# Queries of the next attention core made within the tail of the feed-forward layer before it, and the norm there applied by ScalarE

## The reference, cut to what matters

```python
x = x + tanh(g_xattn[n]) * xattn_n(layernorm(x), ctx)
x = x + tanh(g_ffn[n]) * ffn_n(layernorm(x))
```

## Time and profile before

| | us |
|---|---|
| median of 3 runs | 2401.34 (2396.65 to 2404.51) |
| the profiled execution | 2401.41 |
| its span in the trace | 2399.6 |
| mean granted TensorE clock, share of 2.4 GHz | 0.952 |
| layer 0's feed-forward part: last products end / stage ends | 412.8 / 449.1 |
| layer 2's feed-forward part: last products end / stage ends | 1819.4 / 1833.5 |

### The profile page before, as it was taken

The page is one execution under the profiler, slowest core; times in us unless marked ns, Lnnn a source line. Parts: engine busy times, 40 slices in busy tenths (PEclk is TensorE's granted clock), DMA queues, the critical chain, the costliest instruction groups (busy, mean ns, idle before and its releaser), DMA issues.

```text
span 2399.6 us, 31201 instructions
## 1 busy us (share of the span) xinstructions
PE 2253.9 (94%) x11544; PEld 1565.3 (65%) x11544; DVE 1542.5 (64%) x2508; ACT 1063.7 (44%) x1561; POOL 1397.2 (58%) x887
## 2 busy tenths in 40 slices
PE   6889999899999996698999999989998999999988
PEld 5677887766666653465566665577886666666576
DVE  4666652478788756666778878652224788788652
ACT  3443343355555544311455555443333555555443
POOL 0342200178888875266688888823443788888743
PEclk9899999799999997799899999999998999999989
DMA  1025564211111113100111111022211111111010
GB/s 35 21 67 161 162 194 137 60 40 39 58 39 39 45 54 108 38 1 9 50 59 39 40 58 39 7 78 85 86 34 52 39 39 43 55 39 46 24 39 16
DMA packets 49842, 136.48 MB, mean 57 GB/s; under 512 B 7470, under 2 KB 13438, under 8 KB 49245
## 3 DMA queue, kind: packets, MB, share of 16 engines
q1 hardware_dynamic: 49308, 134.16, 18.3%
q10 hardware_dynamic: 384, 0.33, 0.1%
HBM read 121.26 MB, written 13.21 MB: 56 GB/s over the span
## 4 chain that ended last, share of the span: by engine, by line
PE 83%; DVE 7%; ACT 3%; POOL 3%; DMA 1%; issue 1%; POOLq 0%; ACTq 0%; SPq 0%; DVEq 0%
PE psum L881 21%; PE psum L1315 19%; PE psum L1305 10%; PE psum L1286 10%; PE psum L1307 10%; PE psum L1488 2%; PE psum L1332 2%; PE psum L1443 2%; DMA V<-in_ctx 1%; PE psum L1411 1%; PE psum L1199 1%; PE psum L1511 1%; PE psum L1088 1%; PE psum L1278 1%; PE psum L1108 1%
## 5 line engine op out<-in xcount | busy, mean ns | idle before, releaser
L1741 ACT ACTIVATE E<-psum 125x896 f32<-125x896 f32 x576 | 528.3, 920 | 584.5 <-PE psum L1307 557.9
L2277 DVE TENSOR_REDUCE mx<-psum 128x1 f32<-128x500 f32 x945 | 611.9, 675 | 172.5 <-PE psum L1286 170.6
L2028 POOL TENSOR_TENSOR SA<-SA,E 125x896 f32<-125x896 f32 x282 | 596.9, 2117 | 22.1
L1315 PE MATMUL psum<-E,V 125*64 125x448 f32 x2304 | 472.2, 545 | 0.0
L1305 PE MATMUL psum<-Q,K 128*125 128x448 f32 x1152 | 331.8, 369 | 2.3 <-ACT E L1741 2.3
L1286 PE MATMUL psum<-K,Q 128*128 128x500 f32 x945 | 329.8, 403 | 2.1 <-DVE Q L2217 1.9
L1307 PE MATMUL psum<-Q,K 128*125 128x448 f32 x1152 | 329.9, 367 | 0.0
L1315 PEld LDWEIGHTS psum<-E,V 125*64 125x64 f32 x2304 | 152.9, 136 | 228.5 <-issue 223.2
L2028 POOL TENSOR_TENSOR SA<-SA,SB 125x896 f32<-125x896 f32 x93 | 194.0, 2086 | 154.6 <-DVE SB L2300 154.6
L1286 PEld LDWEIGHTS psum<-K,Q 128*128 128x128 f32 x945 | 174.7, 188 | 133.9 <-DVE Q L2217 32.6
L1305 PEld LDWEIGHTS psum<-Q,K 128*125 128x125 f32 x1152 | 213.2, 187 | 37.1 <-ACT E L1741 6.9
(11 more groups left out here) (308 smaller groups left out, 3703.6 us busy)
## 6 DMA issues: line engine op xcount, KB each, us to landing
K<-kt_scratch SPq DMA_DIRECT2D x48, 750.0 KB, 4.9
K<-kt_scratch SPq DMA_DIRECT2D x48, 375.0 KB, 6.1
EW<-in_f_w SPq DMA_DIRECT2D x64, 256.0 KB, 6.5
kt_scratch<-kt SPq DMA_DIRECT2D x16, 750.0 KB, 4.4
WS<-in_f_w SPq DMA_DIRECT2D x31, 384.0 KB, 5.2
WoT<-in_a_WoT SPq DMA_DIRECT2D x24, 256.0 KB, 2.6
V<-in_ctx SPq DMA_DIRECT2D x16, 375.0 KB
Wq<-in_a_Wq SPq DMA_DIRECT2D x16, 256.0 KB, 3.0
```

The costliest lines, as they stand in the source:

```text
L1315: i = e.matmul(psum[c * DC:(c + 1) * DC, 4 + b % 2, 0:HT], V[0:LP, b, k * DC:(k + 1) * DC], E[g[n, b, k] % NE][0:LP, half[c]], start=k == ...
L1741: e.activation(E[m % NE][0:LP, :].rearrange("p (c q) -> p c q", c=2), psum[0:LP, pair:pair + 2, 0:HT], ACT.Exp).then_inc(exp_set.sem, 1)
L2028: e.tensor_tensor(SA[b % 2][0:LP, :], a[0:LP, :], x[0:LP, :], ALU.add).then_inc(sum_set.sem, 1)
L2277: e.tensor_reduce(mx[:, b % 2, j * 3 + c:j * 3 + c + 1], psum[:, bank, 0:CW], AX.X, ALU.max).then_inc(small_free.sem, 1)
```

## The change

- Core 1 and core 3: the eight makes of c = 0 move out of the core's order into the tail of the feed-forward part before. There they cover the first three token tiles (384 columns), and the eight that stay in the core cover the other four (512 columns; `MADE`). In the tail they use banks 0 and 2, which are free once `OT` has been copied. Make 0 waits for tile 2's `YL`; make mt waits for its folded weights and for ScalarE's copy of make mt - 2.
- The norm in these two tails is applied by ScalarE (`act_norm`: scale and shift by token), with the shift computed by VectorE and GpSimd (`pool_scales` in place of `pool_rstd`), as the other norms of the kernel are.
- Layer 0's tail follows a table, `TAIL`: ScalarE copies both halves to `OT` first (task `ot`), then folding steps, `back`, `stats` (one tile each), `apply`, `norm` and `make` take turns.
- Layer 2's tail: the turns of tiles 0 to 2, 3 and 4, then makes 0 to 3, the turns of tiles 5 and 6, then makes 4 to 7.
- `act_exp_first` runs behind the copy of `OT`'s second half, in the tail.

```diff
--- before.py
+++ after.py
@@ -193,7 +193,7 @@
                 order += side.pop(0)
             if c == 1 and n + 2 < blocks:
                 order.append(("split", n + 2))
-    return order + [("back", 1)]
+    return order + [("back", 1)] + ([("make", mt, 0) for mt in range(4, H // 2)] if blocks == NB2 else [])
 
 
 def folding_ahead():
@@ -255,12 +256,13 @@
             elif g == NG - 1:
                 order += last.pop(0)
     assert not side
-    order.append(("comb", E0 // 2 - 1))
-    for n, task in enumerate([("back", 0), ("back", 1)] + [("norm", i) for i in range(NT)]):
-        for _ in range((3, 3, 3, 1, 1, 1, 1, 1, 1)[n]):
-            order += last.pop(0) if last else []
-        order.append(task)
-    return order + [t for step in last for t in step]
+    order += [("comb", E0 // 2 - 1), ("ot", 0), ("ot", 1)]
+    for folds, tasks in TAIL:
+        for _ in range(folds):
+            order += last.pop(0)
+        order += tasks
+    assert not last
+    return order
 
 
 def core_order(merged):
@@ -270,10 +272,8 @@
 
 
     units = [(j, c) for j in range(NT) for c in range(3)]
-    makes = [("make", 0, mt, c) for c in range(2) for mt in range(H // 2)] if merged else []
-    order = makes[:H // 2]
-    makes = makes[H // 2:]
-    order += [("queries", 0, n) for n in range(6)]
+    makes = [("make", 0, mt, 1) for mt in range(H // 2)] if merged else []
+    order = [("queries", 0, n) for n in range(6)]
     order += makes[:2]
     makes = makes[2:]
     for j in range(NT):
@@ -350,6 +350,11 @@
     return order + [t for step in fold for t in step]
 
 
+TAIL = [(4, [("back", 0), ("stats", 0)]), (1, [("stats", 1)]), (1, [("back", 1), ("stats", 2)]), (1, [("apply", 0), ("stats", 3)]),
+        (1, [("apply", 1), ("norm", 0), ("stats", 4)]), (1, [("apply", 2), ("norm", 1), ("stats", 5)]),
+        (1, [("apply", 3), ("norm", 2), ("stats", 6)]), (1, [("apply", 4), ("norm", 3)]), (1, [("make", 0, 0), ("apply", 5), ("norm", 4)]),
+        (1, [("make", 1, 0), ("apply", 6), ("norm", 5)]), (1, [("make", 2, 0), ("norm", 6)]), (1, [("make", 3, 0)]),
+        (3, [("make", mt, 0) for mt in range(4, H // 2)])]
 SETUP = [("fm", 0), ("turn", 0), ("turn", 1), ("fa", 0), ("turn", 2), ("turn", 3), ("fm", 1), ("turn", 4), ("turn", 5), ("fa", 1), ("turn", 6)]
 FOLD_LOADS = ("fload_r", "fload_m", "fload_a")
 FOLD_BUFS = {1: 4, 2: 1, 3: 1}
@@ -367,6 +372,7 @@
 EARLY_UP = {2: 5, 3: 4}
 LOGITS_BEHIND = {0: 2, 1: 0, 2: 3, 3: 6}
 TURNED_NORM = {0: 1, 2: 5, 3: 8}
+MADE = (slice(0, 3 * P), slice(3 * P, T))
 BACK = {0: ((0, 1), (2,)), 1: ((3, 4), (5, 6))}
 TURNS = {0: (), 1: ((0, 1, 2), (3, 4), (5, 6))}
 
...
@@ -709,7 +715,7 @@
     fm_made, mh_set, ml_set = (flag(n, fm0 + done(folds, "fm")) for n in ("fm_made", "mh_set", "ml_set"))
     fa_made, ah_set, al_set = (flag(n, fm0 + done(folds, "fa")) for n in ("fa_made", "ah_set", "al_set"))
     q_tiles = [(0, mt, c) for mt in range(H // 2) for c in range(2)]
-    q_tiles += [(n, *t[2:]) for n in (1, 3) for t in CORES[n] if t[0] == "make"]
+    q_tiles += [(n, mt, c) for n in (1, 3) for c in range(2) for mt in range(H // 2)]
     q_made, q_set = flag("q_made", q_tiles), flag("q_set", q_tiles)
 
 
@@ -1142,11 +1148,21 @@
                                 t.then_inc(fa_made.sem, 1)
 
     def make_queries(e, n, mt, c, bank):
-        pairs = []
+        pairs, x = [], half[c] if n == 0 else MADE[c]
         for kd in range(KD):
             o = slice(mt * P, (mt + 1) * P)
-            pairs += split_pairs(AH[:, kd, o], AL[:, kd, o], YH[:, kd, half[c]], YL[:, kd, half[c]])
-        product(e, psum[:, bank, 0:HT], pairs).then_inc(q_made.sem, 1)
+            pairs += split_pairs(AH[:, kd, o], AL[:, kd, o], YH[:, kd, x], YL[:, kd, x])
+        product(e, psum[:, bank, 0:x.stop - x.start], pairs).then_inc(q_made.sem, 1)
+
+    def pe_make_ahead(e, f, mt):
+
+        n = f + 1
+        if mt == 0:
+            e.wait_ge(*yl_set.at({0: 2, 2: 6}[f], 2))
+        e.wait_ge(*al_set.at(n, mt))
+        if mt >= 2:
+            e.wait_ge(*q_set.at(n, mt - 2, 0))
+        make_queries(e, n, mt, 0, 2 * (mt % 2))
 
     def pe_queries(e):
         e.wait_ge(*v0_in.at())
@@ -1264,8 +1280,7 @@
         for kind, b, *t in CORES[n]:
             if kind == "make":
                 m = made.index((n, *t))
-                if m >= 2:
-                    e.wait_ge(*q_set.at(*made[m - 2]))
+                e.wait_ge(*q_set.at(*made[m - 2]))
                 make_queries(e, n, *t, 6 + m % 2)
             elif kind == "max_tile":
                 j, = t
@@ -1517,6 +1532,8 @@
                 pe_back(e, f, t[0])
             elif kind == "norm":
                 pe_turn(e, 2, t[0], upper(e, f, "ynorm", t[0]))
+            elif kind == "make":
+                pe_make_ahead(e, f, t[0])
 
     def pe_back(e, f, c):
         for g, group in enumerate(BACK[c]):
@@ -1530,6 +1547,8 @@
                 for i in TURNS[1][g]:
                     pe_turn(e, 6, i, upper(e, f, "ynorm", i))
         if f == 2 and c == 1:
+            for mt in range(4):
+                pe_make_ahead(e, f, mt)
             for i in TURNS[1][2]:
                 pe_turn(e, 6, i, upper(e, f, "ynorm", i))
 
@@ -1701,6 +1720,11 @@
                     e.wait_ge(*valued0.at(p, odd))
                     e.activation(*out0(p, odd, 0), ACT.Copy).then_inc(out0_low.sem, 1)
 
+    def act_made(e, n, mt, c, bank):
+        e.wait_ge(*q_made.at(n, mt, c))
+        x = MADE[c]
+        e.activation(QR[:, mt, x], psum[:, bank, 0:x.stop - x.start], ACT.Copy).then_inc(q_set.sem, 1)
+
     def act_exp_first(e):
 
         e.activation(exp_first[:, :], exponent[:, 0:1], ACT.Exp)
@@ -1709,13 +1733,10 @@
         g = {k: i for i, k in enumerate(per_core("scores"))}
         ks = list(g)
         made = [t for t in q_tiles if t[0] == n]
-        if made:
-            act_exp_first(e)
         for kind, b, *t in CORES[n]:
             if kind == "make":
                 mt, c = t
-                e.wait_ge(*q_made.at(n, mt, c))
-                e.activation(QR[:, mt, half[c]], psum[:, 6 + made.index((n, mt, c)) % 2, 0:HT], ACT.Copy).then_inc(q_set.sem, 1)
+                act_made(e, n, mt, c, 6 + made.index((n, mt, c)) % 2)
             elif kind == "max_tile" and t[0] == 0 and not made:
                 act_exp_first(e)
             elif kind == "queries" and t[0] < 4:
@@ -1794,8 +1815,11 @@
             t.then_inc(part_set.sem, 1)
 
     def act_apply(e, n, i):
-
-        e.wait_ge(*rstd_set.at(1 + 2 * n, i))
+        act_norm(e, 1 + 2 * n, i)
+
+    def act_norm(e, r, i):
+
+        e.wait_ge(*rstd_set.at(r, i))
         e.activation(Y[:, i, :], X[:, i, :], ACT.Identity, scale=rstd[:, i:i + 1], bias=shift[:, i:i + 1]).then_inc(y_set.sem, 1)
 
     def act_project_turn(e, n, i):
@@ -1899,16 +1923,27 @@
                 e.activation(kt[b % 2][0:DC, cols], psum[0:DC, upper_bank[f, (kind, b, g)], 0:4 * LP], ACT.Copy).then_inc(kh_set.sem, 1)
             elif kind in ("fu", "fm", "fg", "fa"):
                 act_fold(e, f, kind, *t)
-            elif kind == "back":
+            elif kind == "ot" or (kind == "back" and f != 0):
                 c, = t
                 e.wait_ge(*(combined.at(E0 // 2 - 1, c) if f == 0 else downed.at(f, FFN_BLOCKS[f] - 1, c)))
                 for k in range(KD):
                     i = e.activation(m["OT"][:, k, half[c]], psum[:, k * 2 + c, 0:HT], ACT.Copy)
                 i.then_inc(ot_set.sem, 1)
+                if f != 3 and c == 1:
+                    act_exp_first(e)
                 if f == 2 and c == 1:
-                    for group in TURNS[1]:
+                    for k, group in enumerate(TURNS[1]):
+                        for i in group:
+                            act_norm(e, 6, i)
+                        if k == 2:
+                            for mt in range(4):
+                                act_made(e, 3, mt, 0, 2 * (mt % 2))
                         for i in group:
                             act_turn(e, 6, i, upper_bank[f, ("ynorm", i)])
+            elif kind == "make":
+                act_made(e, f + 1, t[0], 0, 2 * (t[0] % 2))
+            elif kind == "apply":
+                act_norm(e, 2, t[0])
             elif kind == "norm":
                 act_turn(e, 2, t[0], upper_bank[f, ("ynorm", t[0])])
 
@@ -2091,7 +2126,7 @@
             elif kind == "back" and f != 3:
                 for group in BACK[t[0]]:
                     for i in group:
-                        pool_rstd(e, {0: 2, 2: 6}[f], i)
+                        pool_scales(e, {0: 2, 2: 6}[f], i)
 
     def pool_bits(e):
         for kind, *t in FFN1:
@@ -2145,7 +2180,7 @@
         e.wait_ge(*dve_own.now())
         e.bn_aggr(mv[:, i, :], stats[:, i, :]).then_inc(*dve_own.up())
         e.wait_ge(*dve_own.now())
-        if r in (1, 3, 4, 5, 7):
+        if r > 0:
             e.tensor_scalar(shift[:, i:i + 1], mv[:, i, 0:1], -1.0, None, ALU.mult)
```

(8 more changed lines are left out.)

## The result

The changed kernel took 2386.06 us (median of 5 runs, 2385.07 to 2388.05) against 2402.24 for the kernel before (5 runs, 2396.65 to 2406.01) in the same comparison: ratio 0.9934, 95% interval 0.9918 to 0.9950. The forecast was 2394.0, 7.4 us less than before; measured were 16, over twice as much. Its range (2385 to 2403) holds the value, 1.1 us from its lower end.

A forecast was written before the change was run, and what follows sets the result against it. The prediction took TensorE as the bound (83% of the span). First place -4.2 us (tail +2.5, core -6.7) and second place -3.2 (tail +4.5, core -7.7) took 2401.4 to 2394.0 us; range 2385 to 2403.

The forecast's parts named there:

- Cores: Starts of cores 1 and 3: eight makes leave, keys' wait uncovered, rounds 2.09 us; gains 6.7 and 7.7 us.
- The price of 1.3 us for a fall of the clock in the wait: Each core's wait for keys: TensorE idle some 3.0 us may drop the clock; 1.3 us taken, bounds 0 and 1.7.
- Second tail: Layer 2's tail before core 3: applies move to ScalarE, makes from 1826.4, end 1838.0 against 1833.5; +4.5 us.
- First tail: Layer 0's tail before core 1: two stalls go, eight makes come in; end 451.6 against 449.1, +2.5 us.
- stay low to about 444 in folds, turns and the first makes, and be high in the dense makes behind: First tail: clock at half from about 425.5 to 444, 18.5 us of low-clock work, then 10.7 left taking 5.9 high.
- The step ahead of it: First tail: closed gap lets the clock hold to about 425.5, where VectorE's statistics, additions and copies thin TensorE's work.
- One of my signs of being wrong: Forecast counted as wrong if the first core starts before 446 or after 457.
- the clock holds through the first tail: Rival, 20%: first tail all at high clock, ending 443.7; tail -5.4, core -6.7, total 2386.1 us.
- Low until the last four makes: Rival, 25%: first tail at low clock from 425.5 until the last four makes, ending 454.9; tail +5.8, total 2397.3.
- makes at half clock in both tails: Rival, 6%: the 16 moved makes run at 1.92 us each, not 1.05; first place +4.3, second +1.9, total 2407.6.
- The table's drain: Rival, 4%: the moved Exp table load adds a drain of about 1.38 us; second place 1.4 us worse, total 2395.4.
- three gaps (1.3, 1.8 and a fold of 2.0 us): First tail: TensorE's 1.3 us stall before a turn and 1.8 for a fold's copy go; order ahead by a 1.97 us fold.

The follow-up runs named there:

- OT late: Changed kernel with the first tail's ScalarE copies to OT put back behind folding steps; ratio 0.9936 to the kernel before.
- keys in tail: Changed kernel with VectorE's mask wait moved to its first use and SyncE issuing cores 1 and 3's first keys in the tail before; 2378.3 us, ratio 0.9903.
- the last kernel: Keys in tail plus, in the second tail, makes 0 and 1 and their copies ahead of the turns of tiles 3 and 4; 2375.3 us, ratio 0.9893.
- Makes last: Changed kernel with the first tail's makes 0 to 3 moved behind the last folding steps, all eight makes together at its end; ratio 0.9966.
- mask at use: Changed kernel with VectorE waiting for the block-diagonal mask only at its first use, not ahead of its first reduction; ratio 0.9925.

## Why the prediction was right, and which step was not

**Cores: right to 0.4 us each, core 1 by luck.** The keys landed after 5.5 and 5.4 us (5 to 6 said), TensorE waited 2.50 and 2.40 (3 said), the rounds were 2.08 (2.09). The price of 1.3 us for a fall of the clock in the wait was paid in core 3 (1830.76 to 1834.17), not in core 1. There the unforeseen mask cost 1.3 us in its place (16.4 us behind the first maxima, against 15.1 with neither), which the forecast had at nothing.

**Second tail: right, 0.9 us too long.** On the old time scale (11.45 us later) the addition came at 1821.7 (1821.7 said), the first make at 1826.1 (1826.4), the end at 1837.1 (1838.0). The clock rose 2.4 us into the makes, not 4.4: 2.0 x 0.45 is the 0.9. A still earlier rise gives nothing. In OT late and keys in tail the clock was back before the first make, TensorE then waited 1.22 us ahead of make 2 for ScalarE's copy of make 0, which stands behind the applies, and the tail took the same 19.8 us (the row is OT late's):

```profile
1817.60 0.42 PE L887 MATMUL psum<-YH,AH 128*128 128x384 f32 x1 [1.22 <-ACT QR L1726]
```

In the changed kernel only 0.2 us of that wait are left, since its first makes ran at half clock. Moving the copy is what the last kernel did.

**First tail: the failed step is "stay low to about 444 in folds, turns and the first makes, and be high in the dense makes behind".** The step ahead of it held: on the old time scale the clock fell at 425.5, as put (the two profiles without a fall show that the reason I gave, VectorE thinning TensorE's work, does not settle it). But I sized the low stretch at 18.5 us, because no mix of folds and turns had raised the clock in 29.5 us, and I took only dense makes to raise it. Four makes between folds and turns do so too: the stretch was 6.8 us. The 11.7 us at full clock in place of half save 11.7 x 0.45 = 5.3 of the 6.1 us by which this term is off; the last 0.8 is not explained. One of my signs of being wrong came true with it: core 1 began at 444.42 us, 445.4 on the old time scale, before 446. "Makes last" is what I had priced, without meaning to: its low stretch is 17.1 us and its ratio, 0.9966, times 2401.4 is 2393.2.

**The rivals.** The total is that of "the clock holds through the first tail" (2386.1), but that is not what the profiled execution shows: the clock fell, and the rest of the sum made up for it. It did hold in the profiled executions of two experiments. "Low until the last four makes" and "makes at half clock in both tails" did not happen, since they too left the interleaved makes out. The table's drain was not there. The change did what it says.

**What was missing.** I priced the order by three gaps (1.3, 1.8 and a fold of 2.0 us) and let them hold the clock to 425.5. The fall at 425.5 came out right, but one of the gaps was short (TensorE waited for `OT` twice, 1.4 and 1.3 us), and the largest single part of the gain, 6.7 us in the first tail, thus stood in no line of its own; next to the makes' cost it could not be seen.

## What to carry to other kernels

Where a stretch of small matmuls stands at half clock, the place of the wide ones can count beyond their own cost: here four of eight makes put between the last folds ended it 10 us sooner than all eight behind them. Which matmuls do that has to be read from the clock's row of the stream in question. Work that is moved out of a stage's start uncovers every load that it hid, also those that are waited for early and needed late: list them, move each wait to its use, and issue the first load before the meeting. Two such waits can overlap, so price each with the others gone. When a part of a change is a reordering that looks like the means to the rest, run it alone; here it was nearly half of the gain by the places of the trace (6.7 of 14.7 us) and a third by the ratios.

## What the runs showed that I had not expected

- One kernel's executions differ in where the clock is low. Two profiled first tails had no low stretch (29.6 and 30.7 us); the changed kernel's had one of 6.8 us within 0.3 us of the same point in both of its profiles. A fall of 6.8 us costs 3.1, under half of the spread of the times of one kernel (2380.93 to 2387.89). What decides it was not tested; stretches with the same busy share (2.84 of 3.41 us) were followed by a fall in mask at use and by none in keys in tail.
- A small load issued 1.5 us behind three large ones (`bd`, 24.5 KB, issued at 445.92 us) released its waiter at 453.57, 7.7 us later; the first keys, 750 KB issued ahead of everything, let the first maxima begin 5.3 to 5.8 us after the stage's start with the other loads behind them (7.0 in one core of one run), and landed after 4.3 and 4.2 us alone.
